# Rows past the first 128 of an expert: four column tiles of 32 rows in float32

## The reference, cut to what matters

```python
x2d = x.reshape(bs * slen, dim)                                  # 512 tokens, dim 512
top_scores, token_idx, counts = _route(x2d, gate_w, 8, 2)        # 1024 rows over 8 experts
routed_in = x2d[token_idx] * top_scores[:, None]
for e in range(8):
    h = silu(xe @ w1[e]) * (xe @ w3[e])                          # w1, w3: 512 x 1408
    out = out + h @ w2[e]                                        # w2: 1408 x 512
out = zeros.at[token_idx].add(routed_out)
```

## Time and profile before

| | us |
|---|---|
| median of 3 runs | 1816.54 (1811.77 to 1821.43) |
| profiled execution: its time | 1818.28 |
| profiled execution: its span | 1817.0 |
| TensorE busy in it | 1741.0 |
| VectorE busy | 1086.8 |
| ScalarE busy | 918.9 |
| GpSimd busy | 126.2 |

### The profile page before, as it was taken

One profiled execution on the slowest core, in us unless ns is written; L12 is line 12 of the kernel. 1 busy time (PEld: TensorE's weight loads), 2 busy tenths in 40 slices (PEclk: granted clock), 3 DMA queues, 4 the chain that ended last, 5 costly groups with the idle time before them and its releaser, 6 DMA issues.

```text
span 1817.0 us, 28242 instructions
## 1 busy us (share of the span) xinstructions
PE 1741.0 (96%) x10498; PEld 1333.4 (73%) x10498; DVE 1086.8 (60%) x2297; ACT 918.9 (51%) x1909; POOL 126.2 (7%) x74
## 2 busy tenths in 40 slices
PE   7999999999999999999999999999899879999998
PEld 5778888877888688787777777555455557778787
DVE  5777777764634245555555545787444356775755
ACT  6676666651443234445445444676233345665653
POOL 0000000000000020001000100000111022221222
PEclk9999999998999999999999999999999879999999
DMA  6332222217501698778677767778500347786722
GB/s 230 120 105 82 97 89 93 82 58 271 199 1 36 202 313 273 231 223 240 186 233 225 230 191 224 188 214 266 201 6 7 128 155 257 243 308 199 276 67 64
DMA packets 146710, 309.52 MB, mean 170 GB/s; under 512 B 11424, under 2 KB 100640, under 8 KB 135008
## 3 DMA queue, kind: packets, MB, share of 16 engines
q1 hardware_dynamic: 144640, 301.19, 51.6%
q0 software_dynamic: 1920, 6.36, 1.1%
HBM read 226.75 MB, written 80.76 MB: 169 GB/s over the span
## 4 chain that ended last, share of the span: by engine, by line
PE 85%; DVE 5%; ACT 3%; DMA 2%; issue 2%; DVEq 1%; SPq 1%; POOL 0%; ACTq 0%; POOLq 0%
PE bank L128 15%; PE bank L130 13%; PE bank L129 13%; PE bank L1299 7%; PE bank L1321 5%; PE bank L2200 4%; PE bank L2201 4%; PE bank L2204 4%; PE bank L1675 4%; PE bank L1289 3%; PE bank L1768 2%; PE bank L1332 1%; ACT T L1818 1%; PE bank L1686 1%; PE bank L1755 1%
## 5 line engine op out<-in xcount | busy, mean ns | idle before, releaser
L2501 DVE TENSOR_TENSOR WS<-EW,WS 128x1024 fp32r<-128x1024 f32 (+1 forms) x120 | 148.3, 1242 | 82.8 <-ACT WS L2339 80.5
L1418 DVE CUSTOM_DVE_ANT_0 TT<-bank,MASK 128x512 f32<-128x512 f32 x256 | 174.5, 683 | 22.9 <-PE bank L1289 22.4
L1365 ACT ACTIVATE TT<-TT,MX 128x512 f32<-128x512 f32 x256 | 183.6, 722 | 0.1
L2339 ACT CAST WS<-EW 128x1024 fp32r<-128x1024 f32 (+1 forms) x144 | 139.1, 977 | 64.3 <-PE bank L2204 63.3
L1299 PE MATMUL bank<-IDN,TT 128*128 128x128 f32 x1024 | 159.9, 279 | 0.0
L128 PE MATMUL bank<-BCH,WKT 128*128 128x256 f32 x512 | 154.5, 302 | 4.1 <-DVE BCL L355 4.1
L1431 DVE COPY PT<-bank 128x512 f32<-128x512 f32 x128 | 88.3, 690 | 102.2 <-PE bank L1299 99.3
L130 PE MATMUL bank<-BCH,WKT 128*128 128x256 f32 x512 | 145.4, 284 | 0.0
L129 PE MATMUL bank<-BCL,WKT 128*128 128x256 f32 x512 | 145.2, 284 | 0.0
L1299 PEld LDWEIGHTS bank<-IDN,TT 128*128 128x128 f32 x1024 | 116.0, 140 | 33.0 <-issue 22.2
L1373 ACT COPY PT<-bank 128x512 f32<-128x512 f32 x128 | 75.3, 588 | 113.1 <-PE bank L1299 113.0
(11 more groups left out here) (316 smaller groups left out, 4009.0 us busy)
## 6 DMA issues: line engine op xcount, KB each, us to landing
EW<-in_ewg SPq DMA_DIRECT2D x48, 1024.0 KB, 5.1
KST<-tmp_k SPq DMA_DIRECT2D x43, 768.0 KB, 5.8
tmp_k<-EKH SPq DMA_DIRECT2D x128, 256.0 KB, 2.8
EW<-in_ewg SPq DMA_DIRECT2D x24, 768.0 KB, 4.9
CT<-in_ctxT SPq DMA_DIRECT2D x32, 512.0 KB, 3.5
CN<-in_ctxN SPq DMA_DIRECT2D x32, 512.0 KB, 3.5
BCT<-in_ctxT SPq DMA_DIRECT2D x32, 512.0 KB, 4.2
tmp_k<-EKL SPq DMA_DIRECT2D x64, 256.0 KB, 2.9
```

The costliest lines, as they stand in the source:

```text
L1365: act.activation(TT[:, n % 4, cs], TT[:, n % 4, cs], ACT.Exp, bias=MX[:, n % 4, 5:6], scale=SC1, accum_out=SUM[:, b % 2, h, kc:kc + 1]).th ...
L1418: dve.tensor_tensor_reduce(TT[:, sl, 512 * kc:512 * kc + 512], bank[(0, 1, 4)[g % 3]][:], MASK[:, b % 2, 512 * kc:512 * kc + 512], 1.0, NE ...
L2339: act.copy(WS[:, i % NR, 0, 0:n * w], EW[q % NE][:, at:at + n * w]).then_inc(*w_high.up)
L2501: dve.tensor_tensor(WS[:, i % NR, 1, 0:n * w], EW[q % NE][:, at:at + n * w], f(WS[:, i % NR, 0, 0:n * w]), ALU.subtract).then_inc(*w_low.up)
```

## The change

Block one holds 32 rows (`TAIL = 32`) in place of 128, and works in float32 on the loaded weights EW, without the split:

- its stationary operand is a tile of 128 x 32 tokens, its moving operand 128 columns of EW; four such matmuls with different weight columns write to partitions 0-31, 32-63, 64-95 and 96-127 of one bank (three for the groups that are 384 wide), so its results have the shape 128 x 128;
- SiLU, gate and the copies of block one work on 128 x 128; one transpose turns four hidden blocks; the token and hidden splits of block one (L2511, L2518 for it) go, with their Ifs on VectorE (4 of 7 an expert);
- SyncE loads group q + 12 after TensorE has finished group q (`e_mm[2q+1]`), no more after its split, and stores an expert's rows after its nine groups;
- expert 7's block one is copied to a diagonal buffer YB by two ScalarE and two VectorE copies, and spread with four float32 matmuls in place of eight float32r ones;
- the second gather takes 32 rows; the general path starts past 160 rows (blocks at 160, 288, 416) in place of 256; seven more stores of zeros (256 KB each) stand in the self attention, one more memset on GpSimd.

```diff
+            for e in range(7):
+                sp.dma_start(YD[512 * e + 128:512 * e + 256, :], ZERO[:, 0:512]).then_inc(*st_zero.up)
...
+        TAIL = 32
...
             def group_one(e, g, bk, count):
+                q = 9 * e + g
                 with pe.If(count > 128):
                     if g in (3, 5, 6):
                         n = (g - 2) // 2 if g < 6 else 2
+                        p = TAIL * blocks(n)
                         pe.wait_ge(*gate1(e, n))
-                        hidden(1, n, 6).then_inc(*e_mm1.up)
+                        if n:
+                            pe.wait_ge(*ht1(e, n - 1))
+                        pe.transpose(bank[6][:, 0:p], HH[1][0:p, n % 2, :], IDN[0:p, 0:p]).then_inc(*e_mm1.up)
...
-                    for h in range(2):
-                        if g > 5 and h == 0:
-                            pe.wait_ge(*ht_low1(e, g - 6))
-                        m = times_half(18 * e + 2 * g + h, bank[bk][:, 0:GWIDTH[g]], tokens(1, g, h), h == 0 and g < 7,
-                                       h == 1 and g not in (6, 7))
+                    if g > 5:
+                        pe.wait_ge(*ht1(e, g - 6))
+                    pe.wait_ge(*ld_ew[q % NE][q // NE])
+                    for k in range(GTILES[g]):
+                        rows = XG1[:, k, :] if g < 6 else HT1[:, 4 * (g - 6) + k, :]
+                        for c in range(GWIDTH[g] // 128):
+                            at = k * GWIDTH[g] + 128 * c
+                            m = pe.matmul(bank[bk][TAIL * c:TAIL * c + TAIL, 0:128], rows, EW[q % NE][:, at:at + 128],
+                                          start=(k == 0 and g < 7), stop=(k == GTILES[g] - 1 and g not in (6, 7)))
                     m.then_inc(*e_mm1.up)
...
                 for i in range(4):
-                    spread(1, i, YH, False)
-                    spread(1, i, YL, False)
+                    pe.matmul(bank[SUMS[i]][:], ST[1][:, i, :], YB[:], start=False, stop=False, skip_group_check=True)
...
-                group_one(e, 6, a1, count)
                 split_low(nxt + 12)
...
-            def next_group(i):
-                if i % 2 and i // 2 + NE < 72:
-                    sp.wait_ge(*low_part(i - 1))
-                    sp.wait_ge(*low_part(i))
-                    load_group(i // 2 + NE)
+            def next_group(q):
+                if q + NE < 72:
+                    sp.wait_ge(*e_mm[2 * q + 1])
+                    load_group(q + NE)
...
-            with pe.If(most > 256):
+            with pe.If(most > 128 + TAIL):
```

More of the change, by code:

```diff
@@ L2171, in turn_zero @@
                     pe.wait_ge(*e_index[2 * e + 1])
-                turn(0, 5).then_inc(*e_turn.up)
+                for c in range(4):
+                    m = pe.transpose(bank[5][:, 128 * c:128 * c + 128], HX[0][:, 128 * c:128 * c + 128], IDN[:])
+                m.then_inc(*e_turn.up)
             def turn_one(e, count):
@@ L2184, in turn_one @@
                 pe.end_ifs()
[L2186 to L2189, removed]
             def hidden_zero(e, n):
                 pe.wait_ge(*h_gate[3 * e + n])
-                hidden(0, n, 7).then_inc(*e_hidden.up)
+                for j in range(blocks(n)):
+                    m = pe.transpose(bank[7][:, 128 * j:128 * j + 128], HH[0][:, n % 2, 128 * j:128 * j + 128], IDN[:])
+                m.then_inc(*e_hidden.up)
             def times_half(i, o, a, start, stop):
@@ L2261, in turn_list, with spread @@
                 m.then_inc(*e_listed.up)
-            def spread(v, i, part, stop):
-                return pe.matmul(bank[SUMS[i]][:], ST[v][:, i, :], part[v][:], start=False, stop=stop,
+            def spread(i, part, stop):
+                return pe.matmul(bank[SUMS[i]][:], ST[0][:, i, :], part[:], start=False, stop=stop,
                                  skip_group_check=True)
@@ L2305, in experts_pe @@
                     for i in range(4):
-                        pe.matmul(bank[SUMS[i]][:], ST[0][:, i, :], XG[0][:, 0], start=True, stop=True
+                        pe.matmul(bank[SUMS[i]][:], ST[0][:, i, :], XG[:, 0], start=True, stop=True
                                   ).then_inc(*e_open.up)
@@ L2505, in turn_zero, with hidden_zero @@
                 dve.wait_ge(*x_high[e])
[L2506 to L2516, removed]
+                dve.tensor_tensor(XG[:, 1], bank[5][:], f(XG[:, 0]), ALU.subtract).then_inc(*x_low.up)
+            def hidden_zero(e, n):
                 nj = blocks(n)
[L2518 to L2522, removed]
                 dve.wait_ge(*ht_high[3 * e + n])
[L2524 to L2528, removed]
+                dve.tensor_tensor(HTL2[:, 4 * n:4 * n + nj, :],
+                                  bank[7][:, 0:128 * nj].rearrange("p (a b) -> p a b", a=nj),
+                                  f(HTH2[:, 4 * n:4 * n + nj, :]), ALU.subtract).then_inc(*ht_low.up)
             def gate_zero(e, n, bk):
@@ L2532, in gate_zero @@
                 dve.wait_ge(*h_silu[3 * e + n])
-                gate(0, n, bk).then_inc(*h_gate.up)
+                w = GWIDTH[2 * n]
+                dve.tensor_tensor(HH[0][:, n % 2, 0:w], HS[0][:, 0:w], bank[bk][:, 0:w], ALU.mult).then_inc(*h_gate.up)
             def group_one(e, g, bk, count):
[L2536 to L2540, removed]
-                    with dve.Else():
-                        dve.drain().then_inc(*e_dve1.up)
-                    dve.end_ifs()
                 if g in (1, 3, 5):
+                    p = TAIL * blocks(g // 2)
                     with dve.If(count > 128):
@@ L2839, in far_blocks @@
                 count = load_count(eng, e)
-                for kb in (2, 3):
-                    n = 2 * e + kb - 2
-                    with eng.If(count > 128 * kb):
+                for kb in (1, 2, 3):
+                    n = 3 * e + kb - 1
+                    with eng.If(count > 128 * kb + TAIL):
                         block(e, kb, n)
```

197 lines of the change are left out of this document (101 added, 96 removed).

## The result

| | before | after |
|---|---|---|
| median, us | 1817.99 (4 runs, 1811.77 to 1821.43) | 1760.84 (4 runs, 1758.98 to 1761.93) |
| span of the profiled execution, us | 1817.0 | 1758.9 |

The ratio is 0.9688 (95% interval 0.966 to 0.9717): 57 us faster, where 48 were forecast (1769 us, 8 us too high).

The account below looks back on a forecast made before the run. TensorE was taken as the bound. From 1818.3 us: 46.4 less in four long experts, 1.6 more at the end, 3 less in short experts, 1770.5; median 1.7 lower, 1769 us. Own range 1757 to 1786; 8-in-10 range 1751 to 1795.

Parts of the forecast that it names:

- Block one before, 24.3 us: TensorE, each long expert (1, 4, 6, 7; over 128 rows): block one's matmuls and transposes cost 24.3 us before the change.
- A set at 0.25 us: Block one after: 35 sets of four (or three) column-tile matmuls per long expert, 0.25 us each, 8.75 us; bounds 0.213 to 0.35.
- In and out 0.32 a group: Block one's nine groups: switching tiling costs 0.18 us in and 0.14 out, 2.9 us per long expert.
- Hidden transposes 0.75 and tokens 0.3: Block one after, on TensorE: three hidden transposes at 0.25, 0.75 us, and 32-row token transposes 0.3 us, per long expert.
- VectorE and ScalarE have slack, nothing new is waited for: Long experts: both engines have 10 us of slack; block one's waits lie behind block zero's halves, so TensorE stays the bound.
- The end, +1.6: Block one's last spread: eight float32r matmuls, 1.8 us, become four float32 ones, 3.4 us; 1.6 us slower.
- Short experts, -3: Experts 0, 2, 3, 5 lose four of seven VectorE Ifs: 0.4 us each, 0.5 more for three; 3 us less.
- TensorE's skips: Short experts: skipping block one's larger body on TensorE costs nothing, being covered by matmuls; bound 9 us slower.
- Loads: Expert weights: asking for a group some two groups later leaves over 30 us against 14 for the slowest landing; no cost.
- sets not pipelined (0.53): Rival, block one: each of 35 sets pays 0.53 us, in and out included; 1796 us, chance 11%.
- tiles in series: Rival, block one on TensorE: column tiles run one after another, 32.3 us for 24.3; 1847 us, chance 3%.
- the general path: Rival: expert 7 exceeds 160 rows by rounding and a serial block of some 90 us follows; 1860 us, chance 2%.

Follow-up runs that it names:

- the narrow kernel: Kernel before, with block one's float32r matmuls taking 32 token columns as stationary operand and the same moving columns: 1817.27 us, ratio 1.0008.
- another form (1841.87): Changed kernel with all matmuls of block one sent to the first column tile, one after the other: 1841.87 us, ratio 1.0151.
- the doubled kernel: Changed kernel with every set of four matmuls of block one issued and added up twice: 1799.99 us, ratio 0.9909.

## Why the prediction was right, point by point

The measured 1760.84 us lies inside the forecast's own range (1757 to 1786). The long experts took 37.1 to 37.6 us: within the 36 to 43 that the prediction was staked on, but under the 38 to 40 that it named as likely.

- *TensorE bounds the long experts*: right. Ifs on VectorE left them unchanged, extra sets lengthened them one for one, fewer ways in and out shortened them.
- *Block one before, 24.3 us*: in line with what followed; 50.4 - 24.3 + 11.4 is 37.5, and 37.3 was measured.
- *A set at 0.25 us*: too high. 0.215 to 0.22 was measured, my lower bound. I had added the 0.12 us between two rounds of one lone set; in a stretch it isn't paid. 35 x 0.035 = 1.2 us an expert.
- *In and out 0.32 a group*: 1.01 + 0.20 less four sets at 0.213 to 0.22 is 0.33 to 0.36, right in size. The reason given, a drain at the switch of the tiling, is not shown: narrow tiles alone pay next to none. As the cause is open, that the size was right is luck in part.
- *Hidden transposes 0.75 and tokens 0.3*: three hidden ones at 0.11 and the token transposes at 0.36 in the chain, 0.7 together. So block one is 8 x 1.21 + 1.0 + 0.7, about 11.4, for 12.7; 1.3 us an expert. By the profiles the four long experts gained 4.9 us more than forecast, all of it in experts 1, 4 and 6; expert 7 gained the 11.6 forecast.
- *VectorE and ScalarE have slack, nothing new is waited for*: right in the changed kernel; it ended as soon as groups were run together.
- *The end, +1.6*: 1.6 measured.
- *Short experts, -3*: mis-sized, 5.5 measured. The mechanism (Ifs) is shown, 0.5 us an expert where I took 0.4; but a fall of the clock, some 1.6 us in each of experts 3 and 5, was in the trace as a clock of 0.95 and I gave it no term. It came back in expert 3 with the Ifs, but in expert 3 of the narrow kernel, with its Ifs, it is missing. In the short experts of these profiles each fall stands behind a wait of TensorE for the gate of 1.43 to 1.61 us, none behind 1.1 to 1.2 us, and five waits of 1.41 to 1.60 us had no fall behind them. So the longer wait goes with the fall and does not settle it.
- *TensorE's skips*: that a longer body costs nothing to skip holds for experts 2 and 5, where doubling it changed nothing; expert 3 had a gap of 1 us there. A smaller number of skips was not in my sum: with groups run together TensorE passes 5 fewer and the short experts gained 0.8 to 1.2 us.
- *Loads*: no cost seen, right. The landing stayed at 4.2 to 13.9 us. The later asking and the seven stores were not tested alone.
- *The start of the stage, 3 us*: outside my sum; one execution's share of the clock explains as much, and the change was not shown to have a part.
- *Rivals*: sets not pipelined (0.53) is refuted by 1.01 us for four; tiles in series was shown to be the price of another form (1841.87), close to my 1847; the general path is dearer than priced, 1948 for 1860, and was not entered.

## What to carry to other kernels

A block with few rows costs TensorE its moving columns, not its rows (32 rows in place of 128 changed nothing, ratio 1.0008): to gain from 32 rows, split the weight columns over four column tiles and issue the four neighbours one after the other, with the tile index innermost. Gather such groups, since each way in and out costs about as much as one and a half sets, and look at who is late when you do. An If whose body is skipped is not free on an engine that others wait for; and a capacity that fits the data exactly (160 of 160 rows) stands beside a cliff that should be measured, not guessed.

## What the runs showed of the hardware that I had not expected

- Swapping two loops, same matmuls: 2.39 us a group for 1.01, and 3.61 with all in one tile. TensorE overlaps column tiles partly even where the program does not alternate.
- A single 128x32 tile between 128x128 ones (float32r, 512 or 384 columns) shows no step longer than usual on the way in or out (0.23 us at 512 columns).
- In the doubled kernel TensorE had gaps of 0.3 to 1.1 us without a releaser while eight indirect DMAs were issued, and one of 1.01 us in expert 3, where none was. That its instructions came too late there is a guess that was not tested.
- TensorE fell to 1.2 GHz for some 3.5 us shortly after it had sat idle for 1.4 to 1.6 us and had then done a few transposes, in some executions of the same stretch and not in others (expert 3: 31.52 us with the fall, 29.94 without). Most of the spread of a kernel's time goes with its mean granted clock: the kernel before ran from 1811.5 us at 0.987 to 1818.9 at 0.981, the changed one from 1758.25 at 0.987 to 1762.69 at 0.983. A difference of 3 us between two profiles can be that alone.
